# A new order of the shared expert's pieces and of ScalarE's sixteen steps in a state-space block with routed experts

## What is computed

```python
h = x * rsqrt(mean(x*x) + eps) * norm_scale @ w_in        # 256 -> 2 x 512
xs, res = split(h); res = silu(res)
xs = silu(causal_conv4(xs) + conv_b)
delta, B, C = split(xs @ w_xproj, [16, 32])
delta = softplus(delta @ w_dt + b_dt)
deltaA = exp(delta[..., None] * A)                        # 512 channels x 16 states
deltaBx = (delta * xs)[..., None] * B[:, :, None, :]
ys = scan over time of s = deltaA * s + deltaBx
y = einsum('blcn,bln->blc', ys, C)
x = layernorm(x + x + ((y + xs * D) * res) @ w_out)

normed = x * rsqrt(mean(x*x) + eps) * norm_weight
shared = relu(normed @ sw1 + sb1) @ sw2 + sb2             # 256 -> 1024 -> 256
probs = sigmoid(normed @ router_w.T); scores, idx = top_k(probs, 2)
routed = sum over the two experts e of w_e * (relu(normed @ ew1[e] + eb1[e]) @ ew2[e] + eb2[e])
x = layernorm(x + shared + routed)
```

## Time and profile before

| | |
|---|---|
| three runs, median (lowest to highest) | 1727.56 us (1727.55 to 1731.47) |
| the profiled execution | 1725.55 us |
| its span, first to last instruction | 1723.5 us |
| PE busy (matmuls) | 1483.5 us, 86% |
| DVE busy | 1193.8 us, 69% |
| POOL busy | 952.4 us, 55% |
| ACT busy | 906.6 us, 53% |
| mean granted TensorE clock | 0.914 of full |

### The profile page before, as it was taken

The page is one execution under the profiler, slowest core; times in us unless marked ns, Lnnn a source line. Parts: engine busy times, 40 slices in busy tenths (PEclk is TensorE's granted clock), DMA queues, the critical chain, the costliest instruction groups (busy, mean ns, idle before and its releaser), DMA issues.

```text
span 1723.5 us, 24541 instructions
## 1 busy us (share of the span) xinstructions
PE 1483.5 (86%) x6945; PEld 967.7 (56%) x6946; DVE 1193.8 (69%) x2113; ACT 906.6 (53%) x1778; POOL 952.4 (55%) x590
## 2 busy tenths in 40 slices
PE   7386799989989989989988769967999999999970
PEld 3131235525525525526535326767999999999960
DVE  4499999999999999999999997212333333333327
ACT  4477666777766777665786553212333333333324
POOL 1677797798798798788799884301111111111115
PEclk9697998998998998988999889888999999999995
DMA  5833653455554444534535521936555555555538
GB/s 157 220 94 86 147 135 92 119 131 123 124 127 113 124 120 123 138 96 123 135 94 131 139 67 63 302 103 237 182 179 179 180 179 178 180 180 183 181 126 264
DMA packets 136951, 252.14 MB, mean 146 GB/s; under 512 B 15313, under 2 KB 68418, under 8 KB 136754
## 3 DMA queue, kind: packets, MB, share of 16 engines
q1 hardware_dynamic: 130402, 233.49, 48.6%
q0 software_dynamic: 6480, 17.83, 2.8%
HBM read 205.76 MB, written 45.51 MB: 146 GB/s over the span
## 4 chain that ended last, share of the span: by engine, by line
PE 51%; DVE 26%; ACT 11%; issue 7%; SPq 3%; DMA 2%; POOL 0%; DVEq 0%; ACTq 0%; POOLq 0%
DVE psH L1124 16%; PE psH L1541 15%; PE psP L1552 14%; PE psP L1382 6%; DVE big L1133 6%; PE psP L1371 4%; ACT psH L960 2%; PE psA L1480 2%; PE psA L1461 2%; PE psP L1400 2%; PE psP L1445 2%; SPq L710 1%; PE psA L1471 1%; PE psP L1529 1%; DMA ew_s<-in_L_ffn_ew_dram 1%
## 5 line engine op out<-in xcount | busy, mean ns | idle before, releaser
L472 POOL TENSOR_TENSOR big<-big,B 128x2048 f32<-128x2048 f32 x128 | 578.1, 4530 | 106.1 <-PE psA L1480 51.0
L960 ACT ACTIVATE psH<-big,A_q 128x512 f32<-128x512 f32 x512 | 351.7, 691 | 146.0 <-DVE big L1133 121.5
L1133 DVE TENSOR_TENSOR big<-psH,C 128x512 f32<-128x512 f32 x512 | 350.8, 685 | 0.0
L1124 DVE TENSOR_TENSOR_SCAN psH<-psH,big 128x512 f32<-128x512 f32 x256 | 313.3, 1224 | 50.9 <-ACT psH L960 31.1
L576 POOL DMA_INDIRECT con_dram<-eo,dest x71 | 68.3, 962 | 490.8 <-ACT eo L1032 482.9
L1124 DVE TENSOR_TENSOR_SCAN psH<-psH,carry,big 128x512 f32<-128x512 f32 x256 | 331.8, 1296 | 11.0 <-ACT psH L960 11.0
L1541 PE MATMUL psH<-nTb,ew_s 128*128 128x128 f32 x2272 | 271.4, 279 | 12.9 <-DMA ew_s<-in_L_ffn_ew_dram 8.8
L1541 PEld LDWEIGHTS psH<-nTb,ew_s 128*128 128x128 f32 x2272 | 270.8, 196 | 17.1 <-issue 13.7
L1552 PE MATMUL psP<-big,hT 128*128 x1136 | 257.0, 379 | 0.7 <-DVE eb L1290 0.7
L1480 PE MATMUL psA<-big,gsum 128*32 128x512 f32 x1024 | 218.3, 661 | 44.5 <-DVE big L1133 43.4
L1261 DVE TENSOR_TENSOR hT<-psH,vecs 128x512 f32<-128x512 f32 x142 | 98.2, 692 | 196.4 <-PE psH L1541 196.4
(11 more groups left out here) (173 smaller groups left out, 1544.4 us busy)
## 6 DMA issues: line engine op xcount, KB each, us to landing
ew_s<-in_L_ffn_ew_dram SPq DMA_DIRECT2D x71, 1024.0 KB, 4.8
big<-ud_dram SPq DMA_DIRECT2D x128, 512.0 KB, 8.6
...
B<-bc_dram SPq DMA_DIRECT2D x128, 64.0 KB, 5.7
C<-bc_dram SPq DMA_DIRECT2D x128, 64.0 KB, 5.6
...
```

The lines of the kernel that those rows point to most:

```text
L472: nc.gpsimd.tensor_tensor(X[:, Q % NX], rep[:, g % 2, 1], B4[:, f:f + 1, :].broadcast_to([P, NR, TC]), ALU.mult).then_inc(bx_ready, 1)
L960: nc.scalar.activation(psH[:, r, :], rep[:, g % 2, 0, r, :], ACT.Exp, scale=A_q[:, c, r, f:f + 1]).then_inc(dA_ready, 1)
L1124: nc.vector.tensor_tensor_scan(psH[:, r, :], psH[:, r, :], X[:, Q % NX, r, :], start, ALU.mult, ALU.add).then_inc(scan_done, 1)
L1133: nc.vector.tensor_tensor(X[:, Q % NX, r, :], psH[:, r, :], C4[:, f, :], ALU.mult).then_inc(hc_ready, 1)
```

## The change

`nT`, the shared expert's input rows, gets a buffer of its own instead of `xnT`'s, so its pieces no longer have to be through before the next transposes. They are spread from step 10 of one tile to step 8 of the next, and I 4 to 7 move to steps 11 to 15 and 0. On ScalarE, four decays of each tile, those of r = 2 and 3 at steps 3 and 8 (`AHEAD`), are written to SBUF (`xr` at step 3, `spe` at step 8) right after r = 1 and ahead of the Silu; their scans read the decay there, and in even tiles wait for the copy of the carry, as `psH[:, r]` is written only then. `load_xr` waits for step 3's scans, as it fills `xr`. `add_rows` moves to steps 0 and 9 of the next tile, the SyncE list follows. In the hand-over `LAST` changes, `store_acc` (7, 0) comes before the zero stores and `load_up` (2) before block 3's rows. The 4 MB read of `xall` is cut into 32, one in each pass of two blocks. In the diff, unchanged lines are mostly left out.

```diff
@@ -124,8 +124,7 @@
-        xnT = sb("xnT", [P, DC, TC])
-        nT = xnT
+        nT = sb("nT", [P, DC, TC])
@@ -190,6 +189,7 @@
+        xnT = sb("xnT", [P, DC, TC])
@@ -332,36 +332,38 @@
-        PE_STEPS = {0: ([("D", 2, 0)], [("D", 3, 0), ("N", 5, -2), ("U", 7, -2)]),
-                    1: ([("T", 0, 1)], [("T", 1, 1), ("N", 6, -2)]),
-                    2: ([("O", 0, -1)], [("O", 1, -1), ("N", 7, -2)]),
-                    3: ([("I", 0, 1)], [("I", 1, 1), ("I", 4, 1)]),
-                    4: ([("C", 0, 1)], [("I", 2, 1), ("I", 5, 1)]),
-                    5: ([("C", 1, 1)], [("I", 3, 1), ("I", 6, 1)]),
-                    6: ([("C", 2, 1)], [("I", 7, 1)]),
-                    7: ([("C", 3, 1)], []),
-                    8: ([], [("X", 0, 1)]),
+        PE_STEPS = {0: ([("D", 2, 0)], [("D", 3, 0), ("I", 7, 0)]),
+                    1: ([("T", 0, 1)], [("T", 1, 1), ("N", 4, -2), ("U", 6, -2)]),
+                    2: ([("O", 0, -1)], [("O", 1, -1)]),
+                    3: ([("I", 0, 1)], [("I", 1, 1), ("N", 5, -2)]),
+                    4: ([("C", 0, 1)], [("I", 2, 1)]),
+                    5: ([("C", 1, 1)], [("I", 3, 1)]),
+                    6: ([("U", 7, -2)], [("C", 2, 1)]),
+                    7: ([("N", 6, -2)], [("C", 3, 1)]),
+                    8: ([("N", 7, -2)], [("X", 0, 1)]),
...
-                    11: ([("U", 1, -1)], [("N", 0, -1)]),
-                    12: ([("U", 2, -1)], [("N", 1, -1), ("U", 3, -1)]),
-                    13: ([("N", 2, -1)], [("U", 4, -1)]),
-                    14: ([("N", 3, -1)], [("U", 5, -1)]),
-                    15: ([], [("N", 4, -1), ("P", 0, -1), ("U", 6, -1)])}
+                    11: ([("U", 1, -1)], [("I", 4, 1)]),
+                    12: ([("U", 2, -1)], [("N", 0, -1)]),
+                    13: ([("N", 1, -1)], [("U", 3, -1), ("I", 5, 1)]),
+                    14: ([("N", 2, -1)], [("U", 4, -1), ("I", 6, 1)]),
+                    15: ([("U", 5, -1)], [("N", 3, -1), ("P", 0, -1)])}
...
-        LAST = ([("N", 5, NT - 2), ("O", 0, NT - 1), ("O", 1, NT - 1), ("U", 7, NT - 2), ("N", 6, NT - 2), ("N", 7, NT - 2)] +
-                [(use, i, NT - 1) for use, i in [("R", 0), ("R", 1), ("L", 0), ("U", 0), ("U", 1), ("N", 0), ("P", 0)]] +
+        LAST = ([("O", 0, NT - 1), ("O", 1, NT - 1)] +
+                [(use, i, NT - 2) for use, i in [("N", 4), ("U", 6), ("N", 5), ("U", 7)]] +
+                [("R", 0, NT - 1), ("R", 1, NT - 1), ("L", 0, NT - 1), ("N", 6, NT - 2), ("N", 7, NT - 2)] +
+                [(use, i, NT - 1) for use, i in [("U", 0), ("U", 1), ("N", 0), ("P", 0)]] +
...
-                parts[1].extend([("I", CH, 0), ("I", CH + 1, 0)])
+                parts = (parts[0], [("D", 3, 0), ("I", CH, 0), ("I", CH + 1, 0)])
@@ -392,6 +394,20 @@
         def products(Q, r):
...
             return Q * NR + r + 1
+        AHEAD = (3, 8)
+        def ahead(q, r):
+            return q in AHEAD and r >= 2
+        def decay_of(q, r):
+            if not ahead(q, r):
+                return psH[:, r, :]
+            if q == 8:
+                return spe[:, r - 2]
+            return xr[:, 2 * (r - 2):2 * (r - 1), :].rearrange("p s d -> p (s d)")
...
         def summed(Q):
@@ -647,6 +663,8 @@
+                if k >= 2:
+                    sp.wait_ge(scan_done, ((k - 2) * NQ + 3) * NR + NR)
@@ -678,15 +696,17 @@
+                if k >= 2:
+                    store_acc(k - 2, 0)
+                store_ud(k, 2)
+                load_rep(k, 2)
...
-                store_ud(k, 2)
+                store_ud(k, 3)
+                load_rep(k, 3)
...
-                load_rep(k, 2)
-                store_ud(k, 3)
...
-                load_rep(k, 3)
@@ -699,12 +719,11 @@
-                if k:
-                    store_acc(k - 1, 0)
...
+            store_acc(NT - 2, 0)
@@ -724,6 +743,7 @@
+            store_acc(NT - 1, 0)
@@ -737,13 +757,13 @@
-            for h in range(2):
-                store_acc(NT - 1, h)
+            store_acc(NT - 1, 1)
...
-            load_up(2, 0)
+                if i == 0:
+                    load_up(2, 0)
@@ -754,9 +774,11 @@
-            sp.dma_start(xall[:], acc_dram.rearrange("(t p) d -> p t d", p=P)).then_inc(x_back, 16)
+            acc_rows = acc_dram.rearrange("(t p) d -> p t d", p=P)
+            assert NBLK // 2 - 2 == NSUBS + 1
...
+                sp.dma_start(xall[:, ds(t - 1, 1)], acc_rows[:, ds(t - 1, 1)]).then_inc(x_back, 16)
@@ -915,30 +937,34 @@
-            ACT_STEPS = {(0, 2): [(dt_in, 0, 2)], (0, 3): [(relu_up, -2, 6)],
-                         (1, 0): [(dt_in, 0, 3)], (1, 2): [(relu_up, -2, 7)],
-                         (2, 0): [(read_rows, 1, 0), (dt_exp, 0, 1)], (2, 1): [(read_rows, 1, 1), (dt_ln, 0, 1)],
-                         (2, 2): [(dt_one_plus, 0, 1)], (2, 3): [(dt_less_one, 0, 1)],
-                         (3, 1): [(silu_gate, 0)],
-                         (4, 0): [(read_in, 1, 0)], (4, 2): [(read_in, 1, 1)], (4, 3): [(read_in, 1, 4)],
-                         (5, 1): [(read_conv, 1, 0)], (5, 2): [(read_in, 1, 2)], (5, 3): [(read_in, 1, 5)],
-                         (6, 1): [(read_conv, 1, 1)], (6, 2): [(read_in, 1, 3)], (6, 3): [(read_in, 1, 6)],
-                         (7, 1): [(read_conv, 1, 2)], (7, 2): [(read_in, 1, 7)],
+            ACT_STEPS = {(0, 0): [(relu_up, -2, 5)], (0, 2): [(read_slots, -2)], (0, 3): [(dt_in, 0, 2)],
+                         (1, 1): [(dt_in, 0, 3)], (1, 2): [(read_in, 0, 7)], (1, 3): [(dt_exp, 0, 1)],
+                         (2, 0): [(read_rows, 1, 0), (dt_ln, 0, 1)], (2, 1): [(read_rows, 1, 1), (dt_one_plus, 0, 1)],
+                         (2, 2): [(dt_less_one, 0, 1)], (2, 3): [(relu_up, -2, 6)], (3, 1): [(silu_gate, 0)],
+                         (4, 0): [(read_in, 1, 0)], (4, 2): [(read_in, 1, 1)],
+                         (5, 1): [(read_conv, 1, 0)], (5, 2): [(read_in, 1, 2)],
+                         (6, 1): [(read_conv, 1, 1)], (6, 2): [(read_in, 1, 3)],
+                         (7, 0): [(relu_up, -2, 7)], (7, 2): [(read_conv, 1, 2)],
...
-                         (11, 2): [(one_more, -1), (dt_one_plus, 1, 0)], (11, 3): [(dt_less_one, 1, 0), (relu_up, -1, 0)],
-                         (12, 0): [(relu_up, -1, 1)], (13, 0): [(relu_up, -1, 2)], (13, 2): [(relu_up, -1, 3)],
-                         (0, 1): [(read_slots, -2)], (14, 2): [(relu_up, -1, 4)],
-                         (15, 0): [(norm_row, 2, 0)], (15, 1): [(norm_row, 2, 1)],
-                         (15, 2): [(norm_row, 2, 2), (relu_up, -1, 5)], (15, 3): [(norm_row, 2, 3)]}
-            GATES_0 = {(1, 1): [(read_in, 0, 4)], (1, 2): [(read_in, 0, 5)], (1, 3): [(read_in, 0, 6)],
-                       (2, 0): [(read_in, 0, 7)]}
+                         (11, 2): [(one_more, -1), (dt_one_plus, 1, 0)],
+                         (11, 3): [(dt_less_one, 1, 0), (relu_up, -1, 0)],
+                         (12, 0): [(relu_up, -1, 1)], (12, 2): [(read_in, 1, 4)], (12, 3): [(norm_row, 2, 0)],
+                         (13, 0): [(relu_up, -1, 2)], (13, 2): [(norm_row, 2, 1)],
+                         (14, 0): [(relu_up, -1, 3)], (14, 2): [(read_in, 1, 5)], (14, 3): [(norm_row, 2, 2)],
+                         (15, 0): [(relu_up, -1, 4)], (15, 2): [(read_in, 1, 6)], (15, 3): [(norm_row, 2, 3)]}
+            GATES_0 = {(1, 1): [(read_in, 0, 4)], (1, 2): [(read_in, 0, 5)], (1, 3): [(read_in, 0, 6)]}
+            GATES_1 = {(2, 0): [(read_in, 0, 7)]}
...
-                for part, d, *which in (GATES_0.get(at, []) if k == 0 else []) + ACT_STEPS.get(at, []):
+                steps = ACT_STEPS.get(at, [])
+                if k == 0:
+                    steps = [step for step in steps if step != (read_in, 0, 7)]
+                    steps = steps + GATES_0.get(at, []) if at[0] == 1 else GATES_1.get(at, []) + steps
+                for part, d, *which in steps:
@@ -954,10 +980,13 @@
                 g, Q = k * CH + c, k * NQ + q
                 if f == 0 and r == 0:
                     act.wait_ge(rep_here[g % 2], 64 * (g // 2 + 1))
-                if Q:
-                    act.wait_ge(hc_ready, products(Q - 1, r))
-                keep_state(Q - 1, r)
-                nc.scalar.activation(psH[:, r, :], rep[:, g % 2, 0, r, :], ACT.Exp,
+                if not ahead(q, r):
+                    if Q:
+                        act.wait_ge(hc_ready, products(Q - 1, r))
+                    keep_state(Q - 1, r)
+                elif q == 8 and r == 2:
+                    act.wait_ge(u_ready, (k + 1) * CH)
+                nc.scalar.activation(decay_of(q, r), rep[:, g % 2, 0, r, :], ACT.Exp,
                                      scale=A_q[:, c, r, f:f + 1]).then_inc(dA_ready, 1)
...
             for d in range(DC):
@@ -996,8 +1025,18 @@
             for k in range(NT):
                 for q in range(NQ):
                     for r in range(NR):
-                        decay(k, q, r)
+                        if not ahead(q, r):
+                            decay(k, q, r)
```

(23 more changed lines are left out.)

2 lines of the change are left out of this document (1 added, 1 removed).

## The result

The changed kernel takes 1771.47 us (median of four, 1767.98 to 1774.49) against 1727.97 us, the ratio is 1.0247 with a 95% interval of 1.0223 to 1.027. The forecast was 1751, with a range to 1778. The profiled execution took 1771.3 us, its span is 1769.3.

What follows compares the result with a forecast made beforehand. VectorE was taken to bound the scan stage, TensorE what follows. Stage waits of 80 us for 42 add 38, hand-over and experts give -14.3: 23.5 us more, 1751 us for the median, range 1716 to 1778.

Steps and rivals of the forecast that it cites:

- The lock: Scans with both inputs in SBUF and GpSimd's products block each other, the second to issue waiting fully; 73 us in all.
- Rival A: Scans with both inputs in SBUF do not contend with GpSimd, so both gains come: 1694 us; chance 0.12.
- GpSimd takes its turn with the next 4.53, and VectorE asks 0.59 later: Step 8, tiles 2 to 7: GpSimd's next product runs between the two scans, so the second waits 3.94 us more.
- Step 3: Scans r = 2, 3: 0.8 us each in tiles 2, 4, 6, 2.5 each in 3, 5, 7; 13 in tiles 0 and 1.
- Rival B: One wait per scan pair, as GpSimd gets no turn between the two scans: 1721 us; chance 0.10.
- What is taken away: Scan stage: the new order removes waits for ScalarE's decays at steps 1, 3 and 8; alone, 22 us remain, a gain of 20.
- Tile 0's step 2: Its fourth dt read comes one slot later and delays I5 to I7; the 2.29 us wait grows to about 4.7.
- (f): Hand-over: leftover pieces of tile 6 and N6, N7 before tile 7's first up-projections make the positions 3.6 us later.
- (g): Hand-over: store_acc (7, 0) before the eight zero stores makes block loads 6.2 us later; 3.3 us lost.
- (h): Experts: load_up (2) issued one step earlier removes 4.08 us idle and 1.7 of slow matmuls at block 2.
- (i): Experts: the 4 MB read becomes 32 reads of 128 KB, removing block 5's delay and slow up-projection; 11.8 us saved.
- Rival C: TensorE's order becomes late, O0 and O1 late at steps 2 and 3, 4 us per tile: above 1778; chance 0.06.

Runs made afterwards that it cites:

- held_and_later: `pool_held` with the last two indirect stores of each tile behind product 9 instead of product 8; 1689.23 us, ratio 0.9789 to the kernel before.
- no_ahead: The changed kernel with all decays back in PSUM at their own turn, the new order and hand-over kept; 1696.49 us, ratio 0.9841 to the kernel before.
- pool_held: The changed kernel plus two GpSimd waits per tile, holding products until step 3's and step 8's last scans end; 1702.77 us, ratio 0.9867 to the kernel before.

## Why the prediction was right in sign and 20 us short

- **The lock** ("the one that comes second waits for the whole of the other"). Right that it takes in the scan, that it costs more than all the waits it replaces, and that it decides the sign. Rival A, no contention at 1694, falls. What it would have given is nearest to `held_and_later`, which keeps the SBUF decays with 5.6 us of contention left: 1689. (`no_ahead`, at 1696, is another thing: there the waits behind the Silus are back.) The Trainium skill, SBUF — State Buffer, section "Who interferes with whom", says the same of a VectorE instruction with two SBUF inputs, and that a GpSimd instruction that only writes doesn't contend; by that rule, the trace agrees (4.31 us beside products, 1.23 beside memsets). That section also says that issue order decides who blocks. At 623.58 the scan was issued 0.31 us before the product and waited for the whole of it: there the measurement differs, and it decides.
- **Its size**, 73 us forecast, 99 measured. Tiles 0 and 1 were right: step 3 14.6 for 13, step 8 7.7 for 8. The failed step is "GpSimd takes its turn with the next 4.53, and VectorE asks 0.59 later": in step 8 of tiles 2 to 7 the first scan waits 7.8 to 9.1 us (forecast 2.4 to 3.65) and the second nothing (3.94), 49 us for 42. That the two sums lie near each other is luck, since one wait of up to two products stands where two waits of one were forecast. The turn was read from the last stage, where no store stands before GpSimd's add; it doesn't carry over to products behind a scatter.
- **Step 3** of tiles 2 to 7: 28 us for 10. The argument that r = 3 "falls into the scatter" and costs 0.8 was the larger error: in each of these tiles one scan, asked for 0.2 to 0.3 us before product 5 while the store ahead of it was issued, waits for the whole product, 4.6 to 4.7 us. The store's issue alone holds nothing up (586.25 of `pool_held`).
- **Rival B.** Its sign came in tiles 2 to 7 (at step 8 only the first of the pair is long), its price of 1721 did not: it counted one product in that wait, and there were up to two. Its break-even is also wrong by its own terms: with -6 us for no second wait and eight such waits, the kernel would be no slower below 0.8 us on average, not 2.3. The prediction's test, "if only the first is long, it is B", was too weak, since it didn't ask how long.
- **What is taken away.** 42 us of idle time was to fall to 7 beside the lock; it fell to 8.5. (The waits that the forecast lists without the lock add up to 23 us and not 22; the total doesn't rest on that.) No scan of steps 1, 3 and 8 has a wait in front of it any more. Tile 0's step 2 waits 2.88 us and not 4.7. GpSimd was not late by 1.5 us in tiles 2 and 4: the lock, which in these tiles stops VectorE, gave it 3.4 us of lead.
- **Hand-over.** (f) and (g) were to cost 3.3 us; from the last scan to the first expert's transpose it is 70.6 us for 70.3. That transpose now waits for the block's rows, as foreseen, and no longer for `add_rows`. (h) and (i): 18.6 gained for 17.6 forecast. Block 2's up-projection, 5.44 us after a hole of 4.08, is now 3.73 without a hole:

```profile
1197.77 0.66 PE L1572 MATMUL psP<-ident,xb 128*128 128x128 f32 x2 [6.85 <-DMA xb<-rows_dram]
...
1211.63 3.73 PE L1584 MATMUL psH<-nTb,ew_s 128*128 128x128 f32 x32
```

- **Rival C** (TensorE late, 1778): no; VectorE has 1.0 us of idle time in tile 4, and TensorE its 114.92 us of work. The output projection does come late at steps 2 and 3 of tile 6, by 1.3 us, and in no other tile by more than 0.2.
- **The sum**: stage +63 for +38, hand-over and experts -18.3 for -14.3, hence 1771 for 1751.
